# Two attention layers of a decoder as one software pipeline, with the score and maximum matmuls of a beat in two blocks

## The chip, the cores and the metric

The kernel runs on one core of a Trainium2 chip. The metric is the device time of one execution in microseconds. An execution has a span, from its first to its last recorded instruction; its own time is a little longer. TensorE is PE in the rows (PEld is its weight load), VectorE DVE, ScalarE ACT, GpSimd POOL, SyncE SP; SPq is the queue on which SyncE issues its DMAs.

## The reference

x is 8 batches of 256 tokens with 128 features. Three residual layers follow each other, each on a layer-normalised x:

```python
x = x + attn(layernorm(x), w_qkv, w_out)         # 16 heads of 8, chunks of 64 queries, keys of the chunk and the one before it
x = x + xattn(layernorm(x), ctx, ctx, mask, ...) # 16 heads of 8, 256 queries x 256 keys of the context, with biases
x = x + ffn(layernorm(x), w1, conv_w, conv_b, w2) # quantised linear to 512, depthwise conv of 3, silu, quantised linear back
# both attentions: softmax(q k^T / sqrt(8), masked) v per head
```

## The kernel before

**Units and layers.** The local attention, the cross attention and the feed-forward layer are three stretches of the program, each with a barrier after it. The first two are `attention(False)` and `attention(True)`, with a loop over the 8 batches. A unit, in this text, is one batch in one attention layer: 16 in all, each with two tiles (TPB) of 128 tokens.

**Exact products from bf16.** Each q and k is split into three bf16 parts (high, mid, low), and the parts are stacked in slots of 8 contraction rows, so that one bf16 matmul over 48 rows adds the products that matter. A further row (`MROW`, `MROW + 1`) holds the negated maximum of each query's scores, which is so subtracted inside the matmul, and another the key mask. The kernel builds the slots token by token: ACT casts `high` (L593), DVE makes `rest` (L696) and copies `high` to its slots (`high_stack`, L704), POOL writes mid and low (`split`, L841, L845). Then TensorE turns the stacks, 32 transposes of 128x128 for each unit (`stack_turn`, L346), and ACT (L600) and DVE (L710, L717) copy the result into `QT` and `KT`.

**Maxima ahead of scores.** The maxima need the products with the query on the partition (`max_scores`, L380 in the cross and L384, L390 in the local layer), one bank of 512 columns at a time, which DVE reduces (`max_take`, L732). They are made for batch b + 1 while the scores proper of batch b (`scores`, L415 in the cross and L418, L422 in the local layer, key on the partition) go to ACT's exponential (L615, 1024 columns at once) and on to the product with V (`pv`, L442, L452). When all maxima of a unit are there, `max_turn` (L402) turns them, ACT copies them (L628) and SyncE sends them with two DMAs (L888) into the maximum rows of `QT`. The first scores of the next unit wait for these two.

**Order.** Each engine's order is written by hand in a `step` function for one batch; semaphores tie the engines together. At the start of a step, TensorE turns the stacks of the next batch. SyncE has nothing but the row DMAs to issue between the loads at the start and the stores of the feed-forward layer.

```python
def rows(b, p):
    sp.wait_ge(mT_sb, b + 1)
    for j in range(2):
        sp.dma_start(QT[64 * j + MROW:64 * j + MROW + 1, p, :, j, :],
                     mT[j * PAIRS:(j + 1) * PAIRS, :]).then_inc(m_row, 16)
```

## Time and profile before

| | |
|---|---|
| median of 3 runs | 489.31 us (488.92 to 489.31) |
| the profiled execution | 489.09 us, of which the span is 487.3 us |
| busy | PE 373.3, DVE 302.4, ACT 208.4, POOL 167.2 us |
| the local layer's first maximum rows sent | at 56.44 us |
| the cross layer's first maximum rows sent | at 241.99 us |
| the feed-forward layer starts | at 415 us |

The sends mark the points where each layer's pipeline starts to run full. The time between the first two sends of the table is not all steady work: the local layer drains and the cross layer fills in it.

### The profile page before, as it was taken

To read this page: it belongs to the slowest core of one execution; us is meant where nothing else is said; L and a number is where in the kernel's file an instruction comes from. 1 tells how busy PE (TensorE), PEld (TensorE's weight loads), DVE (VectorE), ACT (ScalarE), POOL (GpSimd) and SP (SyncE) were. 2 spreads that over 40 slices of the span, in tenths; PEclk is the share of its full clock that TensorE was granted. 3 is DMA by queue.
4 is the path that set the end of the run, shared out by engine and by line. 5 is a ranking of instruction groups with operands and counts; after the bars stand their busy time and mean duration, and the time that the engine had idled before them with its cause. 6 is when DMAs were issued, how large, how long until landed. Compare 5 with 4: busy or idle time off the path is not lost. (4 is left out here: it accounts for less than half of the span.)

```text
span 487.3 us, 11267 instructions
## 1 busy us (share of the span) xinstructions
PE 373.3 (77%) x4174; PEld 235.1 (48%) x4174; DVE 302.4 (62%) x710; ACT 208.4 (43%) x296; POOL 167.2 (34%) x242
## 2 busy tenths in 40 slices
PE   0155898898898987625887879797888877399995
PEld 0044566676676665424254544445454543144452
DVE  6285655665665753214866768676677731489975
ACT  1012155445455354312156566556565655133332
POOL 8251431522504313044315233241505191534400
PEclk9987599999999999957599999999999989599998
DMA  8300000000000000000000000000000000000000
GB/s 253 113 0 2 1 3 2 4 3 1 1 0 1 0 1 1 3 0 1 0 2 1 2 3 1 1 0 1 1 0 1 0 1 2 1 5 17 17 24 27
DMA packets 7884, 6.02 MB, mean 12 GB/s; under 512 B 816, under 2 KB 6960, under 8 KB 7856
## 3 DMA queue, kind: packets, MB, share of 16 engines
q1 hardware_dynamic: 6896, 4.07, 2.9%
q10 hardware_dynamic: 960, 1.57, 0.9%
q8 instruction: 18, 0.29, 0.3%
q14 instruction: 10, 0.08, 0.1%
HBM read 4.46 MB, written 1.05 MB: 11 GB/s over the span
## 5 line engine op out<-in xcount | busy, mean ns | idle before, releaser
L732 DVE TENSOR_REDUCE negm<-ps 128x2 bf16<-128x512 f32 (+1 forms) x192 | 123.6, 685 | 24.3 <-PE ps L390 17.3
L615 ACT ACTIVATE probs<-ps 128x1024 f32<-128x1024 f32 x96 | 97.9, 1024 | 47.6 <-PE ps L415 28.2
L841 POOL TENSOR_SCALAR q_stack<-rest 128x512 bf16<-128x512 f32 x18 | 27.8, 1545 | 93.0 <-DVE rest L696 93.0
L380 PE MATMUL ps<-KT,QT 128*128 128x256 bf16 x256 | 47.7, 289 | 13.0 <-DVE negm L732 11.9
L600 ACT COPY QT<-ps 64x1024 bf16<-64x1024 bf16 x32 | 32.2, 1005 | 42.7 <-PE ps L346 42.7
L346 PE MATMUL ps<-identb,q_stack 128*128 128x128 bf16 x256 | 22.9, 242 | 34.4 <-ACT o_sb L622 10.8
L969 PE MATMUL ps<-tapw,xqT 128*128 128x512 f32 x96 | 45.0, 606 | 0.0
L710 DVE COPY QT<-ps 64x1024 bf16<-64x1024 bf16 x32 | 22.2, 695 | 36.0 <-PE ps L346 36.0
L380 PEld LDWEIGHTS ps<-KT,QT 128*128 128x128 bf16 x256 | 18.8, 99 | 44.2 <-DVE negm L732 40.2
L415 PE MATMUL ps<-QT,KT 128*128 128x512 bf16 x128 | 38.5, 385 | 2.1 <-DMA QT<-mT 2.1
L836 POOL TENSOR_TENSOR k_stack<-ones,mask_t 128x32 bf16<-128x32 f32 x9 | 4.0, 447 | 100.4 <-DVE rest L696 100.4
L346 PEld LDWEIGHTS ps<-identb,q_stack 128*128 128x128 bf16 x256 | 17.1, 108 | 42.0 <-issue 29.9
L739 DVE RECIPROCAL rden<-ps 128x16 f32<-128x16 f32 x32 | 8.1, 252 | 45.8 <-PE ps L467 45.8
L442 PE MATMUL ps<-probs,V 128*32 128x256 f32 x512 | 34.2, 385 | 0.6 <-ACT probs L615 0.6
L696 DVE TENSOR_TENSOR rest<-ps,high 128x512 f32<-128x512 f32 x18 | 12.4, 691 | 32.6 <-ACT high L593 32.6
L390 PE MATMUL ps<-KT,QT 128*64 128x128 bf16 x512 | 27.4, 231 | 0.0
L384 PE MATMUL ps<-mask_q,identb 128*128 128x512 bf16 x64 | 25.5, 398 | 2.0 <-DVE negm L732 1.7
L841 POOL TENSOR_SCALAR k_stack<-rest 128x512 bf16<-128x512 f32 x18 | 26.9, 1494 | 0.0
L969 PEld LDWEIGHTS ps<-tapw,xqT 128*128 128x128 f32 x96 | 18.8, 196 | 16.6 <-issue 16.1
L418 PE MATMUL ps<-mask_k,identb 128*128 128x512 bf16 x64 | 24.6, 384 | 2.5 <-DMA QT<-mT 2.5
L390 PEld LDWEIGHTS ps<-KT,QT 128*64 128x64 bf16 x512 | 16.7, 112 | 17.3 <-issue 17.3
L820 POOL TENSOR_TENSOR ve<-mv,eps 128x2 f32<-128x2 f32 x18 | 3.9, 219 | 60.9 <-DVE mv L689 60.9
(161 smaller groups left out, 716.8 us busy)
## 6 DMA issues: line engine op xcount, KB each, us to landing
X<-in_x_dram SPq DMA_DIRECT2D x2, 512.0 KB, 7.5
out_dram<-ob SPq DMA_DIRECT2D x16, 64.0 KB, 1.5
cwb<-in_L_ffn_conv_w_dram ACTq DMA_DIRECT2D x1, 768.0 KB, 8.2
w_sb<-in_L_ffn_w_dram ACTq DMA_DIRECT2D x2, 256.0 KB, 5.6
QT<-mT SPq DMA_DIRECT2D x32, 4.0 KB
cbrow<-in_L_ffn_conv_b_dram ACTq DMA_DIRECT2D x1, 256.0 KB, 8.8
wqkv_sb<-in_L_attn_w_qkv_dram SPq DMA_DIRECT2D x1, 192.0 KB, 9.1
wout_sb<-in_L_attn_w_out_dram SPq DMA_DIRECT2D x1, 64.0 KB, 8.3
```

Source lines behind the costliest of these rows:

```text
L346: last = nc.tensor.transpose(ring(i, BF16)[:, pr * P:(pr + 1) * P], src[:, g:g + 2, :].rearrange("p g c -> p (g c)"), identb[:])
L380: last = nc.tensor.matmul(mb[:, u * S:(u + 1) * S], QT[:, p, pr, j, t * P:(t + 1) * P], KT[:, p, pr, W:W + S], start=True, stop=True)
L384: nc.tensor.matmul(mb, identb[:], mask_q[:, t:t + 1, :].to_broadcast([P, 4, P]), start=True, stop=False, skip_group_check=True)
L390: last = nc.tensor.matmul(mb[W * cc:W * cc + W, u * P:(u + 1) * P], QT[:, p, pr, j, k0:k0 + W], KT[:, p, pr, k0:k0 + P], start=False, stop ...
L415: last = nc.tensor.matmul(o, KT[:, p, g, W + i * P:W + (i + 1) * P], QT[:, p, g, :, :], start=True, stop=True)
L418: nc.tensor.matmul(o, identb[:], mask_k[:, min(g, 1):min(g, 1) + 1, :].to_broadcast([P, 8, W]), start=True, stop=False, skip_group_check=True)
L442: last = nc.tensor.matmul(o[32 * r:32 * r + 32, (i % 2) * S:(i % 2) * S + S], V[:, p, t, h, :], probs[:, h // 2, t * 512 + (h % 2) * S:t * ...
L600: nc.scalar.copy(QT[0:SLOT, p, :, 0, t * P:(t + 1) * P], ring(2 * t, BF16)[0:SLOT].rearrange("p (r s) -> p r s", s=P)).then_inc(qT_even, 1)
L615: nc.scalar.activation(probs[:, g, :], ps[:, k:k + 2, :].rearrange("p a n -> p (a n)"), ACT.Exp, scale=SCALE).then_inc(s_exp, 1)
L732: nc.vector.tensor_reduce(o, src, AX.X, ALU.max, negate=True).then_inc(m_max, 1)
L841: nc.gpsimd.tensor_scalar(slots(stack, *mid), repeated(rest[:, i], mid[2]), 1.0, None, ALU.mult).then_inc(mid_done, 1)
L969: last = nc.tensor.matmul(o, xqT[:, b % 2, t * P + k:t * P + k + P], tapw[:, k, :], start=False, stop=(k == 2), skip_group_check=True)
```

## The change

The two attention layers become one loop over 16 units (`UNITS`), with one set of semaphores and the feed-forward layer behind it. Units 0 to 7 are local, 8 to 15 cross, so that unit 8 is prepared while units 5 to 7 are computed. Weights and inputs come in other layouts, laid out on the host (transposed context, packed weights), so the kernel no longer turns them.

**Beats.** A unit has 8 beats (local) or 16 (cross). A beat (`beat`) issues one bank of score matmuls, then one bank of maximum matmuls, in two blocks (the maxima run one unit ahead of the scores, and three beats more in the local layer, seven in the cross layer), and the classes `Local` and `Cross` say after which beat each other piece of work comes on each engine. The exponential takes 512 columns at a time; scores and maxima have three banks each. Matmuls contract 49 or 50 rows of one half of the partitions (heads 2r in rows 0 to 49, heads 2r + 1 in rows 64 to 113), and the local mask is a matmul after the scores, not before them.

**Stacks by DMA.** Projections are made with the feature on the partition and for two units at once (a group). ACT casts `high`, DVE makes `rest`, POOL `mid` and `low`, once each and with no repeats. SyncE then copies them into the slots of `QT` and `KT`, 24 DMAs for a group (`parts`, `stacks`), each from 64 partitions into 8, 64 KB in all; a cross group has four small ones for the mask besides. No transposes, no copies of stacks on ACT, DVE or POOL are left. The group of units i + 4 and i + 5 is sent at the end of even iteration i, behind the maximum rows of unit i + 1 and ahead of those of unit i + 2.

```diff
-                def stack_turn(b, p, i, free):
-
-                    for s_, v_ in free:
-                        pe.wait_ge(s_, v_)
-                    if i == 0:
-                        pe.wait_ge(highs, 2 * b + 2)
-                        pe.wait_ge(mid_done, 2 * b + 2)
-                        pe.wait_ge(low_done, 2 * b + 2)
-                    src = (q_stack, k_stack)[i % 2]
-                    t = i // 2
-                    for pr in range(PAIRS):
-                        g = t * H + 2 * pr
-                        last = nc.tensor.transpose(ring(i, BF16)[:, pr * P:(pr + 1) * P],
-                                                   src[:, g:g + 2, :].rearrange("p g c -> p (g c)"), identb[:])
-                    last.then_inc(st_ps, 1)
-
...
-                def high_stack(b):
-                    if not (isinstance(b, int) and b == 0):
-                        v.wait_ge(st_ps, 4 * b)
-                    for i, (stack, (first, by, count)) in enumerate(((q_stack, Q_HIGH), (k_stack, K_HIGH))):
-                        dst = slots(stack, first, by, count)
-                        nc.vector.tensor_copy(dst, repeated(high[:, i], count)).then_inc(highs, 1)
-
...
-                        nc.gpsimd.tensor_scalar(slots(stack, *mid), repeated(rest[:, i], mid[2]), 1.0, None,
-                                                ALU.mult).then_inc(mid_done, 1)
-                    for i, (stack, mid, low) in enumerate(((q_stack, Q_MID, Q_LOW), (k_stack, K_MID, K_LOW))):
-                        g.wait_ge(mid_done, 2 * b + i + 1)
-                        nc.gpsimd.tensor_tensor(stack[:, :, low * HD:(low + 1) * HD], rest[:, i],
-                                                stack[:, :, mid[0] * HD:(mid[0] + 1) * HD], ALU.subtract).then_inc(low_done, 1)
...
-        attention(False)
-        attention(True)
...
+def before(u):
+    return 8 * u if u <= B else 8 * B + 16 * (u - B)
...
+def lead_of(u):
+    if u >= UNITS:
+        return 0
+    return 7 if is_cross(u) else 3
+
+
+def max_end(i):
+    return before(min(i + 2, UNITS)) + lead_of(i + 2)
+
+
+def max_range(i, k):
+    first, total, beats = max_end(i - 1), max_end(i) - max_end(i - 1), count_of(i)
+
+    def upto(n):
+        return min(total, n if total <= beats else -(-total * n // beats))
+
+    return range(first + upto(k), first + upto(k + 1))
...
+class Local:
+    PV3, OT0, OT1, V, OT, Y, XT, Q, K, PV0, PV1, MT, PV2 = 0, 1, 1, 2, 3, 4, 4, 5, 5, 6, 6, 6, 7
+    A_O1, A_V, A_OT, A_X, A_HQ, A_HK, A_O0, A_M = 1, 3, 3, 4, 5, 6, 7, 7
+    D_N0, D_N1, D_ST, D_RES, D_RQ, D_RK = 2, 2, 3, 5, 6, 6
+
+
+class Cross:
+    PV3, OT0, OT1, V, OT, Y, XT, Q, K, PV0, PV1, MT, PV2 = 1, 2, 3, 4, 5, 7, 7, 8, 9, 11, 12, 12, 14
+    A_O1, A_V, A_OT, A_X, A_HQ, A_HK, A_O0, A_M = 2, 5, 6, 8, 9, 10, 13, 13
...
+                def beat(i, k):
+
+                    ms = max_range(i, k)
+                    m = ms[0] if len(ms) else None
+                    score_open(i, k)
+                    if m is not None:
+                        max_open(m)
+                    ns = 2 if is_cross(i) else 8
+                    nm = 0 if m is None else 2 if is_cross(max_unit(m)[0]) else 8
+                    for x in range(ns):
+                        last_s = score_mm(i, k, x)
+                    if not is_cross(i):
+                        last_s = score_mask(i, k)
+                    for x in range(nm):
+                        last_m = max_mm(m, x)
+                    if nm == 8:
+                        last_m = max_mask(m)
+                    last_s.then_inc(s_ps, 1)
+                    if m is not None:
+                        last_m.then_inc(m_ps, 1)
+                    for n in ms[1:]:
+                        max_alone(n)
...
+                def iteration(i):
+                    at = places(i)
+                    turn = i + 5 if i + 5 < UNITS else None
+                    grp = (i + 4) // 2 if i % 2 == 0 and (i + 4) // 2 < GROUPS else None
+                    for k in range(count_of(i)):
+                        beat(i, k)
...
+                def split(e):
+                    for n in range(2):
+                        g.wait_ge(rest_done, 2 * e + n + 1)
+                        if e >= 1:
+                            g.wait_ge(st_in[(e - 1) % 3], stacks_in(e - 1))
+                        nc.gpsimd.tensor_copy(mid[:, n, :], rest[:, n, :]).then_inc(mid_done, 1)
+                        g.wait_ge(mid_done, 2 * e + n + 1)
+                        nc.gpsimd.tensor_tensor(low[:, n, :], rest[:, n, :], mid[:, n, :], ALU.subtract).then_inc(low_done, 1)
+
...
+                def parts(g, src, n, slots, done):
+                    dst = KT if n else QT
+                    sp.wait_ge(done, 2 * g + n + 1)
+                    for j in range(2):
+                        for slot in slots:
+                            r0 = 64 * j + HD * slot
+                            o = dst[r0:r0 + HD, g % 3, :, :, W:W + S] if n else dst[r0:r0 + HD, g % 3, :, :, :]
+                            sp.dma_start(o, src[64 * j:64 * j + 64, n, :].rearrange("p (e t) -> p e t", e=2)
+                                         ).then_inc(st_in[g % 3], 16)
+
+                def stacks(g):
+                    if g >= 3:
+                        sp.wait_ge(s_ps, before(2 * g - 4))
+                    if g == 0:
+                        sp.wait_ge(s_dc, V_PADS)
+                    if is_cross(2 * g):
+                        sp.wait_ge(m_in, 32)
+                        for j in range(2):
+                            for e in range(2):
+                                b = 2 * g - B + e
+                                sp.dma_start(KT[64 * j + MASK_ROW:64 * j + MASK_ROW + 1, g % 3, :, e, W:W + S],
+                                             mask_r[:, b * S:(b + 1) * S].unsqueeze(1).to_broadcast([1, PAIRS, S])
+                                             ).then_inc(st_in[g % 3], 16)
+                    for part, (src, done) in enumerate(((high, high_done), (mid, mid_done), (low, low_done))):
+                        parts(g, src, 0, Q_SLOTS[part], done)
+                        parts(g, src, 1, K_SLOTS[part], done)
+
+                def rows(u):
+                    sp.wait_ge(mT_sb, u + 1)
+                    for j in range(2):
+                        sp.dma_start(QT[64 * j + MAX_ROW:64 * j + MAX_ROW + 1, u // 2 % 3, :, u % 2, :],
+                                     mT[j * PAIRS:(j + 1) * PAIRS, u % 2, :]).then_inc(m_row[u % 2], 16)
...
+                stacks(0)
+                sp.dma_start(cwb[:].rearrange("p k c -> p (k c)"), taps_in.to_broadcast([P, 3 * FH])).then_inc(f_in, 16)
+                stacks(1)
+                rows(0)
+                sp.dma_start(wp[:, 4:8, :].rearrange("p n d -> p (n d)"), wpack[:, 4 * D:8 * D]).then_inc(wc_in, 16)
+                sp.dma_start(CT[:], ctx_t).then_inc(c_in, 16)
+                for i in range(UNITS):
+                    if i + 1 < UNITS:
+                        rows(i + 1)
+                    if i % 2 == 0 and (i + 4) // 2 < GROUPS:
+                        stacks((i + 4) // 2)
```

Where the work moves, by engine. On SP, in a local step of the old loop and between two iterations of the new one: of before, the local layer's queue.

```order
16 L888 DMA QT<-mT 1x8x256 x4
17 L893 UNCONDITIONAL_BRANCH
18 L893 ISA
19 L888 DMA QT<-mT 1x8x256 x2
20 L886 REGISTER_ALU
21 L888 DMA QT<-mT 1x8x256 x2
```

Of the changed kernel, the queue from the rows of unit 1 to those of unit 3.

```order
35 L848 DMA QT<-mT 1x8x256 [waits max_copied]
36 L848 DMA QT<-mT 1x8x256
37 L825 DMA QT<-high 8x8x512 [waits high]
38 L825 DMA QT<-high 8x8x512 x5
39 L825 DMA KT<-high 8x16x256 [waits high]
40 L825 DMA KT<-high 8x16x256 x5
41 L825 DMA QT<-mid 8x8x512 [waits mid]
42 L825 DMA QT<-mid 8x8x512 x3
43 L825 DMA KT<-mid 8x16x256 [waits mid]
44 L825 DMA KT<-mid 8x16x256 x3
45 L825 DMA QT<-low 8x8x512 [waits low]
```

Twenty-four DMAs now stand between the maximum rows of two units that follow each other, in every second gap; before, nothing did.

On PE, in the local layer: of before, from the top of a step (the stacks of the next batch, then the first scores).

```order
80 L346 MATMUL ps<-identb,q_stack 128x128 x8
81 L346 MATMUL ps<-identb,k_stack 128x128 x8
82 L337 REGISTER_ALU
83 L346 MATMUL ps<-identb,q_stack 128x128 x8
84 L346 MATMUL ps<-identb,k_stack 128x128 x8
85 L408 ISA
86 L410 ISA
87 L418 MATMUL ps<-mask_k,identb 128x512
88 L422 MATMUL ps<-QT,KT 128x128 x4
89 L418 MATMUL ps<-mask_k,identb 128x512
90 L422 MATMUL ps<-QT,KT 128x128 x4
```

Of the changed kernel, three beats of local iteration 1, with the first product with V of the iteration (L351) and the turn of the next unit's maxima (L328).

```order
102 L290 MATMUL ps<-QT,KT 128x64 x8
103 L296 MATMUL ps<-tri_k,lower 128x512
104 L254 MATMUL ps<-KT,QT 64x128 x8
105 L260 MATMUL ps<-tri_q,twice 128x4x64
106 L351 MATMUL ps<-probs,V 32x64 x32
107 L328 MATMUL ps<-identb,negm 16x128 x2
108 L290 MATMUL ps<-QT,KT 128x64 x8
109 L296 MATMUL ps<-tri_k,lower 128x512
110 L254 MATMUL ps<-KT,QT 64x128 x8
111 L260 MATMUL ps<-tri_q,twice 128x4x64
112 L351 MATMUL ps<-probs,V 32x64 x16
113 L290 MATMUL ps<-QT,KT 128x64 x8
```

The 32 transposes are gone, and only one beat (rows 108 to 112) stands between the turn of the maxima and the next unit's first scores (row 113).

## Rows read from the trace of the kernel before

**Rows 1.** The page: span, engines, slices and granted clock.

```profile
span 487.3 us, 11267 instructions
PE 373.3 (77%) x4174; PEld 235.1 (48%) x4174; DVE 302.4 (62%) x710; ACT 208.4 (43%) x296; POOL 167.2 (34%) x242
```

**Rows 2.** Busy time of each engine in five stretches of the program.

```profile
core 0: us, PE busy (x) PEld busy (x) DVE busy (x) ACT busy (x) POOL busy (x), PEclk, DMA share, GB/s
0.00:56.40 56.40, 21.36 (x154) 14.94 (x155) 33.66 (x60) 6.63 (x10) 26.20 (x40) 0.85 0.26 80
56.40:206.40 150.00, 131.62 (x2322) 96.60 (x2319) 83.90 (x169) 71.77 (x99) 44.20 (x56) 0.99 0.01 2
206.40:242.00 35.60, 18.99 (x102) 10.55 (x103) 17.85 (x38) 5.21 (x10) 14.18 (x21) 0.61 0.00 0
242.00:415.00 173.00, 143.52 (x1346) 83.43 (x1343) 112.27 (x225) 103.25 (x137) 59.63 (x79) 0.98 0.00 1
415.00:487.30 72.30, 57.78 (x256) 29.61 (x256) 54.73 (x218) 21.51 (x41) 23.04 (x48) 0.90 0.05 15
```

**Rows 3.** Timeline of SP: start, duration, the maximum rows of single units.

```profile
74.13 1.31 SPq L888 DMA_DIRECT2D QT<-mT  x2
189.48 1.32 SPq L888 DMA_DIRECT2D QT<-mT  x2
261.73 1.31 SPq L888 DMA_DIRECT2D QT<-mT  x2
395.11 1.32 SPq L888 DMA_DIRECT2D QT<-mT  x2
```

**Rows 4.** Timeline of PE in a local step: start, duration, work.

```profile
142.72 1.14 PE L329 MATMUL ps<-wqkv_sb,xnT 128*128 128x128 f32 x8
143.69 0.38 PE L418 MATMUL ps<-mask_k,identb 128*128 128x512 bf16 x1
143.91 0.39 PE L422 MATMUL ps<-QT,KT 128*128 128x128 bf16 x4
144.13 0.38 PE L418 MATMUL ps<-mask_k,identb 128*128 128x512 bf16 x1
...
145.91 0.65 PE L452 MATMUL ps<-probs,V 128*32 128x64 f32 x32
146.50 0.39 PE L384 MATMUL ps<-mask_q,identb 128*128 128x512 bf16 x1
146.82 0.41 PE L390 MATMUL ps<-KT,QT 128*64 128x128 bf16 x8
147.16 0.39 PE L418 MATMUL ps<-mask_k,identb 128*128 128x512 bf16 x1
```

**Rows 5.** Timeline of PE in a cross step.

```profile
301.18 0.61 PE L380 MATMUL ps<-KT,QT 128*128 128x256 bf16 x4
301.62 0.59 PE L415 MATMUL ps<-QT,KT 128*128 128x512 bf16 x2
...
304.47 1.07 PE L442 MATMUL ps<-probs,V 128*32 128x256 f32 x16
305.45 0.27 PE L402 MATMUL ps<-identb,negm 128*16 128x128 bf16 x2
```

**Rows 6.** Groups by line: busy us, mean ns; idle before and its releaser.

```profile
L732 DVE TENSOR_REDUCE negm<-ps 128x2 bf16<-128x512 f32 x128 | 80.0, 682 | 7.1 <-PE ps L380 5.7
L622 ACT COPY o_sb<-ps 128x512 f32<-128x512 f32 x32 | 18.7, 585 | 12.9 <-PE ps L452 7.0 <-PE ps L442 4.7
L628 ACT COPY mT<-ps 16x256 bf16<-16x256 bf16 x16 | 5.8, 361 | 38.8 <-PE ps L402 38.8
```

**Rows 7.** DMAs: issue in ns (min/median/max), and landing in us.

```profile
L888 SPq DMA_DIRECT2D QT<-mT x32: 634/635/810, 56.4 to 395.8; - x32
L138 SPq DMA_DIRECT2D CTX<-in_ctx_dram x1: 860/860/860, 8.6 to 8.6; - x1
out_dram<-ob SPq DMA_DIRECT2D x16, 64.0 KB, 1.5
q1 hardware_dynamic: 6896, 4.07, 2.9%
```

**Rows 8.** Timeline around the first unit, and the end of the local layer.

```profile
21.27 0.49 DVE L686 BATCH_NORM_STATS2 bnst<-X 128x6 f32<-128x128 f32 x2 [0.61 <-PEq L126]
27.79 0.58 ACT L593 CAST high<-ps 128x512 bf16<-128x512 f32 x1 [2.17 <-PE ps L329]
...
201.14 0.65 PE L452 MATMUL ps<-probs,V 128*32 128x64 f32 x32 [0.53 <-ACT probs L615]
...
205.96 0.42 DVE L747 TENSOR_TENSOR X<-ps,X 128x256 f32<-128x256 f32 x1 [1.71 <-PE ps L486]
```

1340 lines of the change are left out of this document (624 added, 716 removed).

## The prediction

> **What bounds the kernel now.** I read the page first [rows 1]: TensorE is busy for 77% of the span and nothing else for more than 62%. An average over unlike stages says little, so next the stretches [rows 2]. The reader is to see three things. In the local layer (56.4 to 206.4 us) PE is busy for 131.6 of 150.0 us at a granted clock of 0.99: PE's own work sets the pace. In the cross layer (242 to 415) it is 143.5 of 173.0 us, with DVE at 112.3. Between them lie 35.6 us in which no engine works for more than 19.0 us and the granted clock is 0.61, a mean between the levels of 1.2 and 2.4 GHz: the first layer has run dry and the second fills. The feed-forward layer takes 72.3 us and is not changed. Third, the period of a unit from the sends of the maximum rows [rows 3]: (189.48 - 74.13) / 6 = 19.2 us local and (395.11 - 261.73) / 6 = 22.2 us cross. SP has only the two row DMAs to issue in each of them, 1.32 us.
>
> **What a unit costs PE afterwards.** I take start-to-start times, since records overlap. A matmul of 128 columns takes (144.13 - 143.91) / 4 = 0.055 us, one of 512 columns 0.22, and a maximum bank with its change from 128 to 64 output rows 0.32 + 0.34 us, of which about 0.1 is the change [rows 4]. A new local beat is 8 score matmuls of 64 columns, which no row shows: at least half of 0.055, at most 0.055 each, so 0.22 to 0.44; a mask of 512 columns, 0.22; the change, 0.1; 8 maximum matmuls, 0.34; a mask of 256 columns, 0.11. That is 0.99 to 1.21; I take 1.15, since the weight loads are as wide as before, so 9.2 us for 8 beats. The rest: four products with V at 0.59 (146.50 - 145.91), 2.4; the V projection 0.97 (143.69 - 142.72), the q and k projections about the same; and by the same spacing of about 0.11 for each fp32 pass, 8 transposes of o 0.88, three small transposes 0.55 and the output projection 0.45 [rows 4]. Sum 15.4 us. Before, the 32 stack transposes added 32 x 0.055 = 1.8.
>
> A cross beat is four matmuls of 256 columns, 0.44 (301.62 - 301.18), 7.0 us for 16; the products with V 4 x 0.98 = 3.9; the rest 3.5; sum 14.4 us [rows 5]. DVE has 16 reductions of 0.682 = 10.9 and some 3.1 us of other work, 14.0 us: nearly even [rows 6]. Stack copies on DVE and ACT vanish; what they cost hides beside PE's work, and I book nothing for them.
>
> **What is added: DMAs on one queue.** Each group of two units needs 24 stack DMAs of 64 KB, cross groups four small ones more, and the maximum rows of the unit after next are queued behind them. Call d the time that one stack DMA holds this queue. Nothing in the trace is of this kind. Below stands the issue alone: the row DMAs, which also go out in 8 pieces, take 635 ns each and come 0.66 us apart (1.32 for two) [rows 3, 7]. Queue q1 shows 6896 packets of 590 bytes on average; 2.9% of 16 engines' 487.3 us is 33 ns for one [rows 7]. A stack DMA has 64 or 128 pieces; on eight engines 8 x 50 to 16 x 33 ns, 0.4 to 0.5 us, still under the issue. Above stands a store of the same 64 KB that takes 1.5 us from issue to landing [rows 7], if nothing overlaps. An issue with one dimension more took 860 ns [rows 7], and the stack DMAs have such shapes. I take d = 0.8, near the issue rows: bytes alone don't fill the time.
>
> **Where it ends: the chain through the queue.** From the moment t0 at which the maxima of unit i + 1 (i even) are copied: two rows 1.3, then 24d, then (the maxima of i + 2 long ready) two rows 1.3 and a landing of about 1.2 (1.5 less the 0.33 of the store's issue); only then the first scores of unit i + 2 may start. Unit i + 1 itself runs meanwhile: 2.5 us until its rows are there and 15 us of PE, 17.5, against 1.3 + 24d = 20.5. So the queue is later than PE, and the second unit of each pair is free. From the first scores of i + 2 to the copy of the maxima of i + 3 go 15 us (local, at its last beat) or 13.5 us (cross, three beats from the end).
> - Start: input to `high` of the first units takes 7.1 us by the old order (21.27 to 28.37) and the input with DVE's memsets some 10: 17. Then 48 transfers x 0.8 = 38.4 and the rows, 2.5: 58 us, where the old kernel sends its first rows at 56.4 [rows 2, 8]. Unit 0: 15, t0 = 73.
> - i = 0 and 2: 1.3 + 19.2 + 1.3 + 1.2 + 15 = 38.0 each. i = 4: 4 x 0.66 for the mask rows more, 40.6. i = 6, 8, 10: cross, 39.1 each. Together 233.9: 307.
> - What is left of unit 12 is 1.8, units 13 to 15 take 14.4 + 14.4 + about 12 (the last has no maxima to make beside it), small waits 4: 354.
> - The tail, as at the end of the local layer (201.14 to 206.38) 5.3 [rows 8], and the feed-forward layer 72.3 with a barrier [rows 2]: 432 us.
>
> The profiled execution lies 1.8 us over its span and within 0.3 us of the median, so 434 us, against 489.3. What pays is above all the gap between the layers (35.6 us) and pairs at 38 to 41 us in place of 38.4 and 44.4; local pairs gain nothing at this d. The sum holds 48 + 144 = 192 transfers: each 0.1 us of d is worth 19 us, down to d = 0.67, where the queue is no later than PE. The turning point is d = 0.8 + 55/192 = 1.09 us.
>
> **The rivals.**
> - *The transfers hide.* If d is 0.66, SP is done when PE is: the sum falls by 192 x 0.14 = 27 us, to 407. For it: 24 x 0.66 = 15.8 us under a unit of 15.4 plus 2.5. If besides the matmuls of the two partition halves overlap where score and maximum blocks meet, one of four in a cross beat (0.11 x 16 = 1.8 us a unit), the last units win some 7 us: 400.
> - *The destination is the bound (the other side).* Each stack DMA writes 64 KB into eight partitions. If few partitions can't take the data as fast as eight queues bring it, d comes near the 1.5 us of the store. At 1.2 the sum is 434 + 0.4 x 192 = 511, at 1.5 it is 569, and PE stands for 24 x 1.2 + 1.3 - 17.5 = 12.6 us in every pair, after which it starts at 1.2 GHz as in the gap [rows 2] (some 1.5 us for each of 6 pairs, 9 us). It decides from d = 1.09. Against it: no row shows a transfer bound by its partitions, and successive stack DMAs go to different ones. For it: nor does any row show one that isn't.
> - *A wait at each unit's start.* In the local layer the maxima are turned after beat 6 of 8, so their way (an exponential of 512 columns, about the 0.585 of the copy of as many, the copy of the maxima 0.36, two issues 1.3, landing 1.2) outlasts the last beat and the product behind it by about 2.5 us [rows 6, 7]. It is in the sum for the first unit of a pair. If landing takes 1 us more, 8 local and a few cross units pay it: 444.
>
> On the second rival the Trainium skill has a price. SBUF — State Buffer, section Door 1: The DMA port swizzle, says that four neighbouring partitions share a port and gives about 27 GB/s for each; eight partitions are two ports, and 64 KB then take 1.2 us, an estimate from that page that would put the sum at 511 us. No run here shows such a transfer yet; the page measured single large transfers, where all engines write at once, and the queue here moves from port to port.
>
> **How the numbers follow.** My forecast, d between 0.7 and 1.09: 0.50. The transfers hide (395 to 415): 0.20. The destination bounds beyond 1.09: 0.27. Long landings alone: 0.03. Forecast 434 us, its own range 415 to 485. Leaving out the lowest 5 and the highest 12 in 100 gives 398 to 518 us. A difference of 0.2% (1 us) is about what can be told from none. Faster: 0.50 + 0.20 + 0.02 = 0.72; within 0.2%: 0.01; slower: 0.27.
>
> **What would show it.** SP's timeline: stack DMAs 0.8 us apart, and the rows of odd-numbered gaps right behind the 24th. Waits: in every second unit PE on DMA `QT<-mT` for 3 to 6 us; at 12 us or more with SP long idle, the destination is the bound; with SP busy all along, the issue is. PE's clock then dips in those waits. Local beats of 1.15 us and cross beats of 0.44 us without waits show PE's terms. No gap between the layers. It is wrong if PE waits on something else each beat (m_max or s_exp, with one bank of slack less than it seems), or if issues with many pieces take far over 0.86 us.

## The result, and the profile after

The changed kernel takes 566.11 us (median of 4 runs, 563.58 to 574.12) against 489.12 us (488.87 to 489.31): 1.156 times the time before, 95% interval 1.152 to 1.160. In this text medians and ranges hold every execution, while a ratio compares the fast ones alone, since some executions of a kernel are a few per cent slower at a lower clock. I had forecast 434 us and a range of 398 to 518. The sign is wrong, and the time lies outside the range.

The page of the changed kernel, to be read against [rows 1]: the span, the engines, and the granted clock in 40 slices (9 is 90% or more of full speed, 5 is half).

```profile
span 564.8 us, 9996 instructions
PE 401.5 (71%) x3890; PEld 224.3 (40%) x3890; DVE 232.5 (41%) x587; ACT 177.4 (31%) x346; POOL 116.9 (21%) x184
PEclk9755556555655556555656699599769985669998
```

TensorE executes 284 matmuls fewer and is busy 28 us longer. DVE, ACT and POOL lost work (70, 31 and 50 us), as the change intends. The row of clocks is what is new: 5 and 6 from the third slice to the 23rd. The stretches, against [rows 2]: unit 0; units 1 to 6, up to the send of unit 7's maximum rows; units 7 to 12, which are the last local unit and five cross units; the last units; the feed-forward layer.

```profile
core 0: us, PE busy (x) PEld busy (x) DVE busy (x) ACT busy (x) POOL busy (x), PEclk, DMA share, GB/s
61.80:96.30 34.50, 21.43 (x224) 12.13 (x224) 6.65 (x13) 6.92 (x14) 4.97 (x8) 0.55 0.34 55
96.30:281.20 184.90, 157.22 (x1788) 98.29 (x1787) 51.42 (x113) 46.71 (x92) 48.59 (x53) 0.53 0.23 27
281.20:427.00 145.80, 94.04 (x1046) 50.26 (x1046) 73.23 (x141) 62.29 (x125) 17.25 (x24) 0.77 0.28 34
427.00:492.50 65.50, 47.47 (x448) 22.55 (x448) 23.52 (x53) 33.67 (x66) 0.00 (x0) 0.80 0.01 1
492.50:564.80 72.30, 58.44 (x256) 29.87 (x256) 54.17 (x214) 21.51 (x41) 23.09 (x48) 0.90 0.05 15
```

In the local layer PE is busy for 157.2 of 184.9 us at a clock of 0.53; before it was busy for 131.6 of 150.0 at 0.99. It isn't idle and yet runs at 1.2 GHz. Set against the steps of the forecast, the surplus over its span of 432 us is complete: start 61.8 for 58 (+4); unit 0 34.5 for 15 (+19.5); the next six, in three pairs, 184.9 for 38.0 + 38.0 + 40.6 (+68); units 7 to 12, 145.8 for 3 x 39.1 (+28.5); from there to the end 137.8 for 125 (+13). Two thirds of the miss stand in the local layer.

One local beat of the changed kernel, the timeline of PE (start, duration, work), which answers to [rows 4]:

```profile
101.69 0.60 PE L290 MATMUL ps<-QT,KT 50*128 50x64 bf16 x8
102.11 0.61 PE L296 MATMUL ps<-tri_k,lower 64*128 64x512 bf16 x1
102.65 0.64 PE L254 MATMUL ps<-KT,QT 49*64 49x128 bf16 x8
103.22 0.39 PE L260 MATMUL ps<-tri_q,twice 64*128 64x256 bf16 x1
...
150.06 1.92 PE L216 MATMUL ps<-xnT,wp 128*128 128x512 f32 x2
151.90 0.56 PE L290 MATMUL ps<-QT,KT 50*128 50x64 bf16 x8
152.30 0.38 PE L296 MATMUL ps<-tri_k,lower 64*128 64x512 bf16 x1
152.61 0.41 PE L254 MATMUL ps<-KT,QT 49*64 49x128 bf16 x8
152.95 0.28 PE L260 MATMUL ps<-tri_q,twice 64*128 64x256 bf16 x1
```

From start to start the first beat takes 0.42 + 0.54 + 0.57 + 0.32 = 1.85 us. The second comes behind the fp32 projections of q and k (L205, L216: all 128 rows, 512 columns), after which the granted clock stood at 1.0 for about 3 us, from 152.3 on: its score block still took 0.40 at 1.2 GHz, the other three parts 0.31 + 0.34 + 0.19 = 0.84 for 1.43. A score block at a clock of 1.0 is to be seen in the run with full rows and masks below:

```profile
118.75 0.40 PE L292 MATMUL ps<-QT,KT 128*128 128x64 bf16 x8
118.98 0.38 PE L298 MATMUL ps<-tri_k,lower 128*128 128x512 bf16 x1
```

That is 0.23 us, and the whole beat 0.23 + 0.84 = 1.07. My 1.15 was thus a fair price at 2.4 GHz, and the engine wasn't there.

The SP queue, two pieces of its timeline with issues only:

```profile
97.69 3.95 SPq L825 DMA_DIRECT2D QT<-high  x6
112.73 1.29 SPq L825 DMA_DIRECT2D KT<-low  x2
124.47 1.41 SPq L848 DMA_DIRECT2D QT<-mT  x2
...
333.03 2.66 SPq L838 DMA_DIRECT2D KT<-mask_r  x4
350.99 1.29 SPq L825 DMA_DIRECT2D KT<-low  x2
352.33 2.26 SPq L848 DMA_DIRECT2D QT<-mT  x2
```

A stack DMA takes 0.66 us to issue (3.95 / 6), the lower end that I had given. In the local layer SP is done at 114.0 and waits 10 us for the rows. In the cross layer the rows go out right behind the 28th, at 352.33; but PE gets them only at 358.65:

```profile
358.65 0.39 PE L287 MATMUL ps<-QT,KT 50*128 50x256 bf16 x1 [8.23 <-DMA QT<-mT]
358.66 0.39 PE L250 MATMUL ps<-KT,QT 49*128 49x256 bf16 x1
```

With a landing of 1.2 us for the rows themselves, the 24 DMAs of 64 KB, sent from 335.73 on, have taken (358.65 - 1.2 - 335.73) / 24 = 0.91 us each: the data are later than the issue. The same rows show score and maximum matmuls of a cross beat starting 0.01 us apart: they lie in opposite halves of the partitions and run together, as the rival "the transfers hide" had it. Waits of PE, in us: in all, times, longest:

```profile
PE ps L287 <- DMA QT<-mT: 27.6, 8, 12.2
PE ps L365 <- ACT o_sb L510: 12.4, 16, 1.2
PE ps L342 <- ACT o_sb L510: 9.6, 8, 1.4
PE ps L290 <- DMA QT<-mT: 4.7, 5, 1.0
```

Only 4.7 us of waits for rows are left in the local layer: there the slow engine itself hides the transfers.

### The profile page after: what moved, and what is told of

It reads as the page before. It is cut to its first block and busy times, and to the rows that moved or that the text cites. A ratio compares the mean times of both kernels' runs of the same rounds, so it can differ in the third digit from the quotient of the medians.

```text
span 564.8 us, 9996 instructions
## 1 busy us (share of the span) xinstructions
PE 401.5 (71%) x3890; PEld 224.3 (40%) x3890; DVE 232.5 (41%) x587; ACT 177.4 (31%) x346; POOL 116.9 (21%) x184
## 5 line engine op out<-in xcount | busy, mean ns | idle before, releaser
L504 ACT ACTIVATE probs<-ps 128x512 f32<-128x512 f32 x192 | 112.0, 598 | 249.6 <-PE ps L296 160.8
L287 PE MATMUL ps<-QT,KT 50*128 50x256 bf16 x256 | 47.0, 302 | 30.2 <-DMA QT<-mT 27.6
L290 PE MATMUL ps<-QT,KT 50*128 50x64 bf16 x512 | 38.5, 236 | 20.8 <-issue 15.2
L250 PE MATMUL ps<-KT,QT 49*128 49x256 bf16 x256 | 51.4, 311 | 0.4 <-DVE negm L608 0.4
L254 PE MATMUL ps<-KT,QT 49*64 49x128 bf16 x512 | 40.0, 307 | 16.3 <-DMA KT<-low 13.7
L290 PEld LDWEIGHTS ps<-QT,KT 50*128 50x128 bf16 x512 | 29.4, 123 | 40.9 <-issue 33.0
L287 PEld LDWEIGHTS ps<-QT,KT 50*128 50x128 bf16 x256 | 16.8, 98 | 57.7 <-DMA QT<-mT 29.7
L365 PE MATMUL ps<-identf,o_sb 128*128 128x128 f32 x128 | 29.9, 394 | 12.4 <-ACT o_sb L510 12.4
L296 PE MATMUL ps<-tri_k,lower 64*128 64x512 bf16 x64 | 38.2, 597 | 0.0
L351 PE MATMUL ps<-probs,V 128*32 128x64 f32 x1024 | 29.2, 289 | 12.1 <-ACT o_sb L510 5.5
L351 PEld LDWEIGHTS ps<-probs,V 128*32 128x32 f32 x1024 | 23.8, 153 | 19.0 <-ACT o_sb L510 8.2
L342 PEld LDWEIGHTS ps<-probs,V 128*32 128x32 f32 x512 | 14.4, 118 | 27.1 <-ACT o_sb L510 12.0
```

Of the source, the lines that this page charges most:

```text
L250: return nc.tensor.matmul(o[:, x * S:(x + 1) * S], QT[r, s, pr, e, t * P:(t + 1) * P], KT[r, s, pr, e, W:W + S], start=True, stop=True)
L254: return nc.tensor.matmul(o[W * cc:W * cc + W, x // 2 * P:(x // 2 + 1) * P], QT[r, s, pr, e, k0:k0 + W], KT[r, s, pr, e, k0:k0 + P], start ...
L287: return nc.tensor.matmul(o[:, x * S:(x + 1) * S], KT[r, s, pr, e, W + kt * P:W + (kt + 1) * P], QT[r, s, pr, e, :], start=True, stop=True)
L290: return nc.tensor.matmul(o[:, x * W:(x + 1) * W], KT[r, s, x, e, W * c:W * c + P], QT[r, s, x, e, W * c:W * c + W], start=(x == 0), stop= ...
L296: return nc.tensor.matmul(bank(n % 3).rearrange("p (r q) -> p r q", q=W), lower[64 * j:64 * j + 64, :], tri_k[64 * j:64 * j + 64, :].unsqu ...
L342: last = nc.tensor.matmul(o[32 * r:32 * r + 32, n % 2 * S:(n % 2 + 1) * S], V[:, i % 2, kt, 4 * n + r, :], probs[:, 4 * n + 2 * kt + r % 2 ...
```

## The experiments

Eighteen kernels ran, on the chips that also ran the kernel before (489.4 to 490.1 us). The runs with full rows and those on what a stack DMA waits for don't compute the reference's output; they are there for their timing. The theories: A, the clock of the local layer is held down by the matmuls of the beat, which fill 49 or 50 of the array's 128 rows; B, by the short waits of about 1.3 us at turns and projections; C, the transfers are the cost.

**The order: alternating in place of blocks.**

```diff
-                    for x in range(ns):
-                        last_s = score_mm(i, k, x)
...
-                    for x in range(nm):
-                        last_m = max_mm(m, x)
+                    for x in range(max(ns, nm)):
+                        if x < ns:
+                            last_s = score_mm(i, k, x)
+                        if x < nm:
+                            last_m = max_mm(m, x)
```

> One part of the change undone: a beat issues score and maximum matmuls in turn, one of each, and the two masks behind them. Theory A (in the local layer TensorE runs at 1.2 GHz because of the kind of matmuls it has: half of the array's rows, 64 columns; order plays no part in it): the clock stays at 0.5 there, but neighbours now lie in opposite halves of the partitions and overlap, so that the 0.42 and 0.57 us of the two blocks become about 0.6 together; a local beat goes from 1.9 to about 1.5 us, 64 of them give some 25 us: about 540 us. The cross layer stays, since its two score and two maximum matmuls overlap already. Theory B (the clock is held down by waits of about 1.3 us at turns and projections and by the rows behind the stacks; order plays no part): the same 540 us, clock 0.5. Rival C (the blocks themselves are what holds the clock down, because alternating pairs would fill both halves of the array): clock 1.0 in the local layer, beat about 0.8 us, unit 18 us: 566 - 7 x 12 = about 480 us.

Measured: 682.56 us (676.98 to 687.08), 1.392 times before. All three expectations fell. The timeline of PE:

```profile
102.00 0.20 PE L290 MATMUL ps<-QT,KT 50*128 50x64 bf16 x1
102.13 0.24 PE L254 MATMUL ps<-KT,QT 49*64 49x128 bf16 x1
102.30 0.20 PE L290 MATMUL ps<-QT,KT 50*128 50x64 bf16 x1
...
109.90 0.23 PE L290 MATMUL ps<-QT,KT 50*128 50x64 bf16 x1
110.31 0.23 PE L290 MATMUL ps<-QT,KT 50*128 50x64 bf16 x1
```

The first rows lie in a short stretch at a granted clock of 1.0, the last two at 0.5. A score matmul and a maximum matmul take 0.41 us in turn at 1.2 GHz, where blocks take 0.42 / 8 + 0.57 / 8 = 0.12, and 0.30 at 2.4 GHz, where blocks take 0.23 / 8 + 0.34 / 8 = 0.07: over three times as much at either clock, though they lie in opposite halves. One has 128 outputs, the other 64. Where both have 128, in the cross layer, the starts are 0.01 us apart in either order. The number of columns isn't it either: in one beat of this run local scores of 64 columns alternate with cross maxima of 256, both with 128 outputs, and two of them start together.

```profile
402.55 0.23 PE L290 MATMUL ps<-QT,KT 50*128 50x64 bf16 x1
402.55 0.39 PE L250 MATMUL ps<-KT,QT 49*128 49x256 bf16 x1
```

So the cost goes with the change of output count, as far as these rows tell; no run changes that count alone. [Rows 4] show it once per bank, here it comes at every matmul. The rows of unit 6 leave at 352.7 us in place of 247.4: 105 of the 120 us between the two profiled executions are lost by then, in the local layer. Against strict alternation the blocks are worth 116 us to this design; they aren't why it lost.

**The clock: masks over 128 rows, a filler, full rows.**

```diff
-... twice[64 * j:64 * j + 64, :], tri_q[64 * j:64 * j + 64, :] ...
-... lower[64 * j:64 * j + 64, :], tri_k[64 * j:64 * j + 64, :] ...
+... twice[:], tri_q[:] ...
+... lower[:], tri_k[:] ...
```

> The two mask matmuls of a local beat contract all 128 partitions in place of 64 (the mask's value is doubled by it, nothing else changes): same count, same columns. Theory A: the engine's array is filled more and the granted clock of the local layer rises from 0.53; if it rises to 1.0, a unit falls from 30.7 to about 18 us and the whole to 480 us; if half of the time, 520. Theory B (waits): clock and time stay, 566 us within 1%. Theory C (transfers): the same as B.

Measured: 574.88 us (572.57 to 577.6), 1.177 times before; the clock between the rows of units 0 and 8 is 0.54 (0.53 unchanged). Masks alone do nothing.

```diff
+                    if not is_cross(i):
+                        nc.tensor.matmul(<score bank>, identb[:], <onesb, 512 columns>, start=True, stop=True, ...)
```

> Work added: ahead of the scores of each local beat one bf16 matmul of identity and ones, 128 rows by 128 outputs by 512 columns, into the bank that the scores then start anew (64 in all, result not used). Theory A: they lift the clock of the local layer; at 2.4 GHz they cost 0.22 us each, a beat is about 1.35 us in place of 1.9, a unit about 20 us: 566 - 7 x 10 = about 495 us. Theory B and C: clock stays at 0.5, each filler costs 0.43 us: 566 + 64 x 0.43 = 594 us, slower.

Measured: 598.18 us (569.07 to 601.56). In the profiled execution (601.3 us) each filler took 0.57 us from start to start and the clock stayed at 0.54, as B and C had it. But one of the four executions took 569.07 us, with a mean clock of 0.74 over its whole span against 0.67 to 0.69 in the other three. It has no trace that would say where it gained, so whether one matmul of full rows in a beat can lift the local clock stays open.

```diff
-                r = slice(64 * j, 64 * j + ROWS + 1)     # maxima; scores: ROWS + 2
+                r = slice(0, P)                          # local units only
```

> Score and maximum matmuls of the local units contract all 128 partitions in place of 49 or 50 of one half (each then sums two heads; the exponential is scaled down so that it stays finite, and memsets of the unused rows delay the start by 10 to 20 us). Count, columns, order and semaphores stay. Theory A (half-filled array): the granted clock of the local layer is 1.0 after its first units, a local beat takes 1.0 to 1.2 us, the sends of odd units lie about 40 us apart, not 61.5. Theory B (waits of 1.3 us and the turns between keep the clock down): clock 0.5 to 0.55 and 61 us for two units as before, since a matmul of the same columns costs the same whatever its rows.

> As the run with full rows (scores and maxima contract all 128 partitions and sum two heads, exponential scaled down, start delayed by memsets), and the two masks over 128 partitions too, so that every matmul of a local beat fills all rows as in the kernel before. That run had a clock of 0.77 between 102 and 237 us, in turns of 1.0 and 0.50; masks alone had changed nothing (0.54). Theory A (rows filled decide): the clock is 0.9 or more between the first rows and the last local unit, a unit about 19 to 21 us. Theory B (short waits throw it back whatever the matmuls): 0.7 to 0.8 as before.

Besides the rows, the edit clears the unused rows with memsets and scales the exponential down. Measured: full rows 581.11 us (one run), full rows and masks 560.46 us (558.85 to 562.07), both with a start 30 us later than the changed kernel (the memsets). The stretch from the rows of unit 0 to those of unit 8, eight local units, in the changed kernel, with masks alone, with full rows, and with both:

```profile
61.80:306.40 244.60, 199.09 (x2266) 123.67 (x2266) 69.12 (x150) 60.55 (x118) 59.68 (x67) 0.53 0.27 34
```

```profile
61.80:313.90 252.10, 205.44 (x2266) 126.11 (x2266) 69.34 (x150) 60.68 (x118) 59.61 (x67) 0.54 0.26 33
```

```profile
91.60:308.70 217.10, 167.19 (x2266) 110.81 (x2266) 69.28 (x151) 60.41 (x118) 59.59 (x67) 0.69 0.27 37
```

```profile
91.50:284.30 192.80, 129.14 (x2274) 87.28 (x2278) 69.11 (x151) 60.00 (x118) 59.60 (x67) 0.85 0.28 40
```

The same 2266 matmuls (2274 in the last stretch) with the same columns and the same order: PE is busy for 199, 205, 167 and 129 us at clocks of 0.53, 0.54, 0.69 and 0.85. These means lie between what the two theories expected: full rows alone were to give 1.0 by A and 0.5 to 0.55 by B, full rows and masks 0.9 or more by A and 0.7 to 0.8 by B. One unit decides. Unit 1, from the send of its rows to that of unit 2's, in the changed kernel and in the run with full rows and masks:

```profile
96.30:124.50 28.20, 25.18 (x299) 16.44 (x298) 7.39 (x18) 7.26 (x16) 12.08 (x12) 0.50 0.49 58
```

```profile
111.84:130.02 18.18, 14.02 (x298) 10.08 (x298) 7.30 (x18) 7.00 (x15) 7.82 (x9) 1.00 0.51 62
```

In the second the clock is 1.00 throughout, though PE still stands twice for 1.3 us in it, once for the rows and once for `o_tok`. That is theory A, and B falls. Behind it the longer waits for rows grow (17.7 us in 5, against 4.7) and the clock falls to 0.80 and 0.87 over the next two pairs: as soon as PE is fast, the transfers are late. Units 0 and 1 of the last run took 20.3 and 18.2 us, the pace of the old kernel's 19.2 [rows 3]; the pairs behind took 52.5 and 54.8.

**The transfers: rows on another queue, and fewer of them.**

```diff
+                    for j in range(2):       # in the copy of the maxima on ACT
+                        act.dma_start(QT[64 * j + MAX_ROW:..., u // 2 % 3, :, u % 2, :],
+                                      mT[j * PAIRS:(j + 1) * PAIRS, u % 2, :]).then_inc(m_row[u % 2], 16)
```

> The two DMAs of a unit's maximum rows are issued by ACT right behind its copy of the maxima, not by SP behind 24 stack DMAs. ACT has 1.3 us more to issue per unit. Transfer theory (the queue is what I got wrong): the 27.6 us that PE waits for the rows in the cross layer mostly go, and with them the 1.2 GHz stretches behind them (about 9 us in each of 4 gaps, at half speed: 4 x 4.5 = 18), so 566 - 25 - 18 = about 520 us. Theory A: the same in the cross layer, nothing in the local one, where SP waits for ACT already: 520 to 535. Theory B: the local clock rises too, to about 480 us. If the rows wait for the data in front of them in the 16 engines and not for the issue, moving them to another queue gives less than 10 us: 556 to 566.

> As the run with the rows on ACT's queue, but issued behind the copy of o, not ahead of it: in that run PE waited 39 us for o_sb (L510) in 16 waits of up to 3.2 us, against 15 before. If those waits were all that made it slower than the changed kernel, they go, and the rows no longer wait behind stacks in the cross layer: 566 - 20 = 546 us. If the rows still land late because the 16 engines are full of stack data, 560 to 570 us.

Measured: 590.16 us (588.4 to 595.51, ratio 1.211) and, issued behind the copy of o, 578.32 us (578.03 to 581.18, ratio 1.182). Both are slower than the changed kernel, and than anything that I had expected. In the first PE waits 39 us for `o_sb` ahead of its products with V where it waited 15; the second removes that, but 36 us of waits for the rows remain, against 32.3. They have moved: 13.1 us in the cross layer for 27.6, where the rows no longer stand behind 24 issues, and 22.9 in the local layer for 4.7. There the rows of unit 1 go out on ACT's queue at 91.02 us, in the middle of a group that SP issues until 99.1, and PE gets them at 99.67; those of unit 2, with no stacks under way, go out at 125.31 and are there at 127.81. So another queue doesn't bring rows past data that are already under way (8.7 us for 2.5), while in the cross layer the issue order held them too.

```diff
-                        for slot in slots:
+                        for slot in slots if g < 3 else slots[:(len(slots) + 1 - j) // 2]:
```

> From group 3 on only 12 of the 24 stack DMAs of a group are sent (60 of 192 left out; the other slots keep the data of three groups before, so the output isn't the reference's). It prices the transfers. My prediction's step has each cost 0.8 us on the path: 60 x 0.8 = 48 us less, 518. If they matter only in the cross layer, where PE waits for the rows (27.6 us in 8 waits, and a slow clock of some 9 us behind each of 4 of them): 566 - 25 - 4 x 4.5 = about 523 us. If the waits of PE move to what stands next (o_sb, X, o_tok), less than 15 us: over 550. Local units stay at 30.7 us each by either.

Measured: 545.89 us (541.5 to 552.2), ratio 1.112, above the 518 and 523 of the two main expectations. The waits of L287 fall from 27.6 to 5.7 us, and two local units still take 61.7 us. The 60 DMAs are worth 20 us, 0.34 us each and not 0.8: in the local layer nothing; in the cross layer the waits for rows.

**What a stack DMA waits for.**

```diff
-                    for j in range(2):
+                    for j in range(2 if g < 3 or n == 0 else 0):      # K only: n == 1
...
+                            if g >= 3 and slot < 5:                   # third run
+                                sp.dma_start(wide[64 * j:64 * j + 64, slot, :], src[64 * j:64 * j + 64, n, :]
```

> The changed kernel, but from group 3 on only the 12 Q stacks of a group are sent (pieces of 1 KB, 64 for each DMA; the K slots keep old data, so the output isn't the reference's). If the drain goes by bytes or by the destination, the data move at the same 65 GB/s as in the full groups and as with K alone. If it goes by pieces, Q alone moves at the pace of its issue, 99 GB/s, and K alone at 50 GB/s or less.

> The changed kernel, but from group 3 on only the 12 K stacks of a group are sent (pieces of 512 bytes, 128 for each DMA; the Q slots keep old data, so the output isn't the reference's). By pieces: 50 GB/s, 1.2 to 1.3 us for each DMA. By bytes or destination: 65 GB/s, 0.96 us, as for Q.

> The run with Q stacks only, but from group 3 on 10 of the 12 DMAs of a group (high and mid) write their 64 KB into the 64 partitions they come from, in a buffer that nothing reads, not into 8 partitions of QT; same bytes, same 1 KB pieces, same issue. If the eight partitions written are what holds a stack DMA to 65 to 70 GB/s, the data now flow at the pace of the issue, 99 GB/s, and the 10 are done about 1 us after the last issue, in place of 3 us. If engines or the source are the limit, the rate stays at 65 to 70.

One window of 1 us in the middle of one group: Q only, K only, and Q into 64 partitions (the last column is GB/s, the one before it the share of the 16 DMA engines).

```profile
164.00:165.00 1.00, 1.00 (x10) 0.50 (x9) 0.00 (x0) 0.63 (x2) 0.00 (x0) 0.50 0.61 72
```

```profile
164.00:165.00 1.00, 1.00 (x33) 0.83 (x25) 0.30 (x1) 0.00 (x0) 0.00 (x0) 0.50 0.65 64
```

```profile
164.00:165.00 1.00, 1.00 (x31) 0.80 (x21) 0.26 (x1) 0.00 (x0) 0.00 (x0) 0.50 0.48 105
```

Times (one run each): 543.45, 551.26 and 544.31 us; what counts here are the rates. Q in pieces of 1 KB moves at 65 to 72 GB/s, K in twice as many pieces of 512 bytes at 60 to 65: pieces matter little. Into 64 partitions, with all else as for Q, 87 to 124 GB/s in the four windows from 164 to 168, mean 106, at a smaller share of engine time: the pace of the issue, 64 KB in 0.66 us being 99. The spread over partitions goes with the rate, and a stack DMA takes 64 KB / 68 GB/s = 0.96 us. But the run with 64 partitions changes a second thing: in its trace the stack semaphores get 16 completion updates for each wide DMA (as for each store of 64 KB) and nine for each stack DMA, so the wide ones seem to be shared out over more DMA engines as well. Whether the eight partitions written or the fewer engines hold a stack DMA isn't shown; the rival "the destination is the bound" fits, below its turning point. SBUF — State Buffer, section Door 1: The DMA port swizzle, of the Trainium skill gives 27 GB/s for each port and so 54 for eight partitions; the trace has 60 to 72 for a stream of such DMAs that moves on from one set of eight partitions to the next. By the page's figure d would be 1.2, by the trace it is 0.96.

**Beats in pairs, so that halves overlap.**

```diff
+                    for x in range(8):
+                        score_mm(i, k, x)
+                        score_mm(i, k + 1, x)
+                    score_mask(i, k).then_inc(s_ps, 1)        # masks over 128 rows
+                    score_mask(i, k + 1).then_inc(s_ps, 1)
...                                                            # the maxima of two beats likewise
```

> Local beats two at a time: the 16 score matmuls of two beats in turn (opposite halves of the partitions, same 128 outputs by 64 columns), both masks (over all 128 partitions), then the 16 maximum matmuls of two beats in turn (64 outputs by 128 columns), both masks. Neighbours of one shape in opposite halves should overlap as the cross layer's do: two beats cost 0.42 + 2 x 0.54 + 0.57 + 2 x 0.32 = 2.7 us in place of 3.8 at 1.2 GHz, 32 of them save 35 us: 531. The switch between shapes, which made the alternating order slow (0.30 us for a pair against 0.12), is paid once in two beats. Theory A: with both halves filled the clock rises as well, two beats 1.4 us at 2.4 GHz, and PE is then bound by the three banks and by exponential and reduction, a unit about 18 us: 566 - 7 x 12 = about 480 us, below the kernel before. Theory B: only the overlap, 525 to 540 us.

> On the paired beats: the stack DMAs of a part go out slot by slot with the two partition halves in turn, not three slots of one half and then three of the other. In the paired run the data flow at 60 to 70 GB/s while DMAs into one half follow each other (24 DMAs drained in 23 us, 0.96 us each) and at 98 to 112 GB/s at the end of one group, where the halves alternate. If the half read from or written to is the limit, 24 DMAs drain at the pace of their issue, 0.66 us, rows land 7 us earlier in each odd gap: 532 - 7 x 7 = about 485 us. If it is the engines' time for each piece (the DMA share is 0.6 to 0.65 throughout), the rate stays at 65 GB/s and the time at 532 us.

> On the paired beats: half of the stack DMAs left out from group 3 on (old data in the other slots, so the output isn't the reference's). 12 drain in 11.5 us, well under a unit. It shows what is left when the transfers are hidden: if they are the bound of the paired version, 430 to 460 us and a clock near 1.0 from unit 5 on; if TensorE's own work and short waits are, 500 us or more.

Measured: 531.89 us (528.69 to 534.04), ratio 1.086 [1.081, 1.090], so 34 us less than the changed kernel. That time is what theory B expected of the overlap alone (525 to 540, A: 480); the trace below says why it isn't B. With the halves of the DMAs in turn 527.29, ratio 1.081 [1.072, 1.090]: the intervals overlap, so no effect of the order of halves is shown. With half of the transfers left out 483.86, ratio 0.979 [0.973, 0.986], against an expected 430 to 460: they are left out from group 3 on only, and of the 28.7 us of waits for rows in the local layer 24.8 remain. PE in the paired run:

```profile
153.62 0.41 PE L290 MATMUL ps<-QT,KT 50*128 50x64 bf16 x16
153.96 0.60 PE L296 MATMUL ps<-tri_k,lower 128*128 128x512 bf16 x2
154.49 0.42 PE L254 MATMUL ps<-KT,QT 49*64 49x128 bf16 x16
```

Sixteen score matmuls of two halves take 0.34 us at 2.4 GHz, where a block of eight takes 0.23. The clock of the local layer now goes to 1.0 between waits (0.70 in the mean from 61.8 to 275 us), and the waits are for the rows, in the local layer too:

```profile
PE ps L290 <- DMA QT<-mT: 28.7, 6, 14.3
PE ps L287 <- DMA QT<-mT: 28.1, 8, 12.2
```

Leaving out 60 transfers is worth 48 us here, 0.80 each, and 20 us in the changed kernel: transfers cost about what I predicted only once PE isn't slower. That it is just 0.8 is chance, since the 48 us hold the slow clock behind the waits as well.

**Transfers spread, and a version that beats both.**

```diff
-                        stacks((i + 4) // 2)                  # 24, behind the rows of unit i + 1, i even
+                        stacks((i + 4) // 2, i % 2)           # 16 behind these, 8 behind the rows of i + 2
```

> The changed kernel with blocks as they are, and only the stack DMAs spread 16 and 8. The local layer is bound by TensorE at 1.2 GHz there and SP has slack: nothing gained. In the cross layer the 27.6 us of waits for rows and the slow clock behind them go, as with half of the transfers left out (20 us less): about 545 us. If it gives more than 30 us, the transfers cost the changed kernel more than that run showed.

> On the paired beats: 16 stack DMAs of a group stay behind the rows of the first unit, 8 go behind those of the second, so that no rows stand behind more than 16. If the transfers on the queue are what bounds the paired version (56.8 us of PE waiting for rows in 14 waits of up to 14.3 us, each followed by some 9 to 16 us at 1.2 GHz): 16 x 0.96 = 15.4 us drain under a unit of about 18, the waits shrink to a few us in all, the clock of both layers stays near 1.0: 532 - 50 - 30 = about 450 us, faster than before. If PE's clock falls for another reason (waits of 1.3 us), 532 - 50 = 480 us. If the second part comes too late for the maxima of the next group, PE waits for KT<-low instead: 510 us or more.

> Paired beats, stack DMAs spread 16 and 8 and with the halves in turn, and in the cross layer the turns of o, the V projection, oT, y, x, q and k and the last product with V each one beat later, so that PE doesn't stand for o_sb (9.6 us in 8 waits and half of 14.9) and oT (5.7). Against the spread run (486 us): 10 to 20 us less if these waits are on the path, 466 to 476; the same 486 if DVE's 16 reductions of 0.68 us and its small work bound the cross unit.

> The version with paired beats, spread transfers and the later turns of the cross layer; the rows of unit 0 now go out behind 16 of the 24 stack DMAs of group 1, and the load of the cross layer's weights and of the 1 MB context behind the stacks of group 2, not right behind the first rows. In the spread run the rows of unit 0 were sent at 61.8 us and the first scores began at 73.7, while 118 to 146 GB/s of context and stack data passed. If the rows stand behind that data, the first scores begin at 61 to 65 us and the whole falls by 8 to 12 us, to 474 to 478. If unit 1's or 2's maxima then wait for the rest of group 1 or the context is late for unit 8, the gain is under 3 us.

Measured: spread alone on the changed kernel 558.43 us (554.95 to 563.74), ratio 1.137, 8 us less where I expected 21; its waits of L287 fall from 27.6 to 14.3 only. On the paired beats 486.39 us (479.85 to 500.06), ratio 0.987 [0.983, 0.991]: 1.3% faster than before, and 45 us less than the paired run, where I had expected about 450 us. The later turns bring nothing that can be told from it (485.31, 468.68 to 488.0); the waits for `o_sb` fell by 4 us, those for `oT` not at all. What stood out was one row of the waits of the spread run, in both versions:

```profile
PE ps L290 <- DMA QT<-mT: 23.2, 6, 14.1
```

The 14.1 us are those of unit 0, whose rows stand behind the stacks of group 1 and beside the 1 MB context. With 16 stacks ahead of these rows and the context later, on top of the pairs, the spread and the later turns, 471.49 us (467.98 to 488.62), ratio 0.957 [0.953, 0.962]: the best version of this study, 4.3% below the kernel before. The first scores begin at 65.1 us in place of 73.5, which is the part that was expected. The median falls by 14 us where 8 to 12 were expected, but the quickest execution with the later turns alone took 468.68, so the size of this last step can't be told from the scatter. Its page:

```profile
span 470.2 us, 9997 instructions
PE 315.4 (67%) x3886; PEld 172.9 (37%) x3890; DVE 229.2 (49%) x587; ACT 174.9 (37%) x346; POOL 116.7 (25%) x184
PEclk9965559699996968695779979996999976699998
```

PE is busy 86 us less than in the changed kernel for the same matmuls, which is overlap and clock together; the clock is 0.83 in the mean, and 28 us of waits for rows are left.

## Why the prediction was wrong

**The step that failed** is "A local beat ... That is 0.99 to 1.21; I take 1.15, so 9.2 us for 8 beats", and with it "Sum 15.4 us". The durations came from rows at a granted clock of 0.99 and were carried over to matmuls of another shape as if the clock came with them. It didn't: PE was busy for 26.4 us in a unit, not 15.4 (52.73 in the 61.6 us of two units). Of these 11 us the beats make 8 x (1.85 - 1.15) = 5.6; the other matmuls of the unit ran at 1.2 GHz too. At 2.4 GHz the sum was sound: a beat takes 1.07 us, and unit 1 with full rows and masks kept PE busy for 14.0. The runs show which part of the change does it. The same matmuls over all 128 rows take a third less time at 0.85 (129 for 199 us), while masks over 128 rows alone (0.54), or half of the transfers left out (0.53 to 0.55), leave the clock where it was. The kernel before contracts 128 rows in these matmuls [rows 4]. TensorE: Matmul & The Clock Gate of the Trainium skill, section Part 1, says that "the default state is throttled, and activity releases the throttle", and I read activity as being busy, so I gave a slow clock no rival of its own except behind long waits. Here the engine was busy for 85% of 184.9 us and stood at 1.2 GHz nearly throughout, while the same matmuls with all rows filled ran at 0.85 in the mean, busy for only 67% of their stretch (129.14 of 192.80). So being busy isn't enough, and the measurement decides.

**d, one stack DMA, 0.8 us:** the term was mis-sized, not misconceived. The issue is 0.66 and the transfer 0.96, both within the bounds that I gave (0.66 and 1.5). With 0.96 the sum would have been 434 + 0.16 x 192 = 465 us, still faster. Its place was wrong as well: nothing of it is on the path in the local layer of the changed kernel, where 1.2 GHz covers it, and all of it is once the clock is repaired.

**The cross layer, 39.1 us a pair:** 48.6 measured over units 7 to 12. The wait in each odd gap is there, 4.3, 8.2 and 12.2 us for the 3 to 6 that I expected, and behind it PE's clock dips, for which I booked nothing in the likeliest case; besides, PE waits in every cross unit for `o_sb` twice (1.1 and 1.2 us) and for `oT` (0.7), which "small waits" didn't hold.

**Slower, with a chance of 0.27,** isn't a hit: that chance stood on a destination bound beyond d = 1.09, which measured 0.96, and not on the clock of the local layer.

**Right:** the gap between the layers is gone; DVE's, ACT's and POOL's savings hide; the start at 58 us (61.8); an issue of 0.66 us as the lower end of d [rows 3, 7]; halves that overlap in a cross beat, though only in a rival.

**The title's order** isn't what failed: in turn it would have been 683 us. It isn't the best order either, since pairs of beats took 532.

## What to carry to other kernels

A row gives a duration at a clock. Before a duration is carried over to matmuls of another shape, ask whether the clock will come along: work that fills half of the array's rows can cost twice as much in the end, and a bound of twice the time belongs in the range. When rows are halved, issue matmuls of the two halves in turn and with the same output count, so that they overlap (0.34 us for 16 at 2.4 GHz, against 0.23 for a block of 8); in turn with another output count they cost over three times what blocks did here. A queue of transfers is priced by how fast their data move as well as by their issue (0.96 and 0.66 us here), and data that something urgent follows are to be sent in portions shorter than the work they hide beside.

## What the hardware showed that I had not expected

- TensorE at a mean clock of 0.53 for 185 us while busy for 85%, with bf16 matmuls of 49 and 50 rows; 0.85 of full speed with 128 rows, and 1.00 over a whole unit with two waits of 1.3 us in it.
- Two matmuls in opposite halves overlap when both have 128 outputs (starts 0.01 us apart), and cost 0.41 us a pair at 1.2 GHz, against 0.12 in blocks, when one has 128 and the other 64 (0.30 against 0.07 at 2.4 GHz).
- A stream of DMAs of 64 KB into eight partitions moves at 60 to 72 GB/s, into 64 partitions at 106, about the pace of its issue (0.66 us, 99 GB/s). The first get nine completion updates each and the second 16, so the number of DMA engines may be the cause as well as the partitions.
- Why full rows still left 0.85, and not 0.99 as before, stays argued: the longer waits for rows go with it, but no run took all waits away.
